# Spreading the inverse softmax sums of two later attentions through DRAM, in a three-part transformer kernel

## What is computed

```python
x = layernorm(x + attn_block(x))          # 16 heads of 16, window 128, then an MLP of 1024
y = x
for l in range(2):                        # the two later layers
    h = shift_token(y)                    # half of the columns come from the token before
    q, k, v = split(h @ wqkv[l], 3)       # 8 heads of 64
    q, k = l2norm(q) * qs[l], l2norm(k) * ks[l]
    q, k = rotary_xpos(q, k)
    o = local_attention(q, k, v)          # softmax over the window before and the window itself
    y = y + o @ wo[l]
    h = layer_norm(shift_token(y)) @ w1[l] + b1[l]
    a, g = split(h, 2)
    y = y + (a * gelu(g)) @ w2[l] + b2[l]
x = layernorm(x + y)
```

## Time and profile before

| | |
|---|---|
| time of the runs | 1791.54 us median of 3 (1789.31 to 1791.67) |
| the profiled execution | span 1791.1 us; its own time is not given apart, the median is 0.4 us above the span |
| TensorE busy | 1731.2 us (97%) |
| VectorE busy | 1494.1 us (83%) |
| ScalarE busy | 1197.5 us (67%) |
| GpSimd busy | 1080.0 us (60%) |
| DMA queue of SyncE | 20.5% of 16 engines' span |
| granted TensorE clock | 9 tenths or more in all slices |

### The profile page before, as it was taken

One profiled execution on the slowest core, in us unless ns is written; L12 is line 12 of the kernel. 1 busy time (PEld: TensorE's weight loads), 2 busy tenths in 40 slices (PEclk: granted clock), 3 DMA queues, 4 the chain that ended last, 5 costly groups with the idle time before them and its releaser, 6 DMA issues.

```text
span 1791.1 us, 43798 instructions
## 1 busy us (share of the span) xinstructions
PE 1731.2 (97%) x15424; PEld 1496.0 (84%) x15424; DVE 1494.1 (83%) x3797; ACT 1197.5 (67%) x3088; POOL 1080.0 (60%) x1060
## 2 busy tenths in 40 slices
PE   6999999999999999999999999989999999999997
PEld 4778777789998888888887888878888888888886
DVE  6888988868878898888987678789898898967776
ACT  6999988854445787877876334358787877743332
POOL 3676556534434778778773455377878777634343
PEclk9999999999999999999999999999999999999999
DMA  3111211032322111111112434331111111131221
GB/s 107 38 37 38 67 44 31 26 107 75 108 63 99 48 41 54 44 52 51 44 43 71 147 105 126 100 103 41 52 44 55 41 54 47 31 102 56 82 82 36
DMA packets 139812, 116.03 MB, mean 65 GB/s; under 512 B 10584, under 2 KB 138848, under 8 KB 138848
## 3 DMA queue, kind: packets, MB, share of 16 engines
q1 hardware_dynamic: 139616, 113.53, 20.5%
HBM read 75.74 MB, written 37.75 MB: 63 GB/s over the span
## 4 chain that ended last, share of the span: by engine, by line
PE 84%; DVE 9%; ACT 3%; issue 3%; POOL 0%; DMA 0%; SPq 0%; DVEq 0%; POOLq 0%; ACTq 0%
PE psum L567 17%; PE psum L569 17%; PE psum L568 17%; PE psum L906 6%; PE psum L874 5%; PE psum L887 5%; PE psum L682 3%; PE psum L664 3%; PE psum L848 3%; ACT a_probs L1718 2%; PE psum L920 2%; PE psum L617 1%; DVE a_neg_max L1211 1%; DVE psum L1209 1%; PE psum L654 1%
## 5 line engine op out<-in xcount | busy, mean ns | idle before, releaser
L1837 ACT ACTIVATE b_probs<-masked,neg_max 128x256 f32<-128x256 f32 (+1 forms) x512 | 250.6, 494 | 124.3 <-DVE neg_max L1343 124.3
L1343 DVE CUSTOM_DVE_ANT_0 masked<-psum,mask 128x256 f32<-128x256 f32 (+1 forms) x512 | 177.3, 412 | 75.9 <-PE psum L874 75.9
L567 PE MATMUL psum<-wa_hi,b_h_hi 128*128 128x512 f32 (+1 forms) x576 | 233.8, 406 | 6.9 <-DVE wa_lo L1138 3.9
L568 PE MATMUL psum<-wa_lo,b_h_hi 128*128 128x512 f32 (+1 forms) x576 | 214.0, 372 | 0.0
L569 PE MATMUL psum<-wa_hi,b_h_lo 128*128 128x512 f32 (+1 forms) x576 | 214.0, 372 | 0.0
L567 PE MATMUL psum<-g_h_hi,wm_hi 128*128 128x512 f32 (+1 forms) x480 | 190.5, 397 | 2.7 <-POOL g_h_lo L2121 1.6
L2070 POOL TENSOR_TENSOR g_in<-g_in,minus_half 128x16 f32<-128x16 f32 x64 | 188.2, 2940 | 4.5 <-DVE g_in L1295 4.5
L568 PE MATMUL psum<-g_h_lo,wm_hi 128*128 128x512 f32 (+1 forms) x480 | 189.3, 394 | 0.0
L569 PE MATMUL psum<-g_h_hi,wm_lo 128*128 128x512 f32 (+1 forms) x480 | 189.2, 394 | 0.0
L1458 POOL TENSOR_TENSOR g_in<-g_z,g_in 128x512 f32<-128x512 f32 x62 | 79.8, 1287 | 143.4 <-DVE g_in L1289 138.2
L567 PE MATMUL psum<-wm_hi,u_hi 128*128 128x256 f32 x576 | 164.3, 285 | 0.1
(11 more groups left out here) (169 smaller groups left out, 5644.0 us busy)
## 6 DMA issues: line engine op xcount, KB each, us to landing
x_mid<-y_out SPq DMA_DIRECT2D x96, 128.0 KB, 1.7
rope_in<-in_rope SPq DMA_DIRECT2D x64, 128.0 KB, 2.2
x_res<-x_state SPq DMA_DIRECT2D x64, 128.0 KB, 2.2
g_in<-x_mid SPq DMA_DIRECT2D x32, 256.0 KB, 3.8
g_old<-x_state SPq DMA_DIRECT2D x16, 512.0 KB, 4.0
out_x<-g_fin SPq DMA_DIRECT2D x15, 512.0 KB, 2.9
w_raw<-in_w_mlp_b SPq DMA_DIRECT2D x2, 2154.0 KB, 8.8
x_in<-in_x SPq DMA_DIRECT2D x32, 128.0 KB, 2.2
```

The lines of the kernel that those rows point to most:

```text
L567: nc.tensor.matmul(out, a_hi, b_hi, start=first, stop=False)
L568: nc.tensor.matmul(out, a_hi, b_lo, start=False, stop=False)
L1343: ins = nc.vector.tensor_tensor_reduce(out[:, at], src[:, at], (mask if now else mask0)[:, at], -1.0, BIG, ALU.add, ALU.min, neg_max[:, r, ...
L1837: ins = nc.scalar.activation(out, src, ACT.Exp, bias=neg_max[:, r, k:k + 1], scale=-1.0, accum_out=row_sum[:, n % 2, 4 * r + k:4 * r + k + 1])
```

## The change

The GpSimd copy, the four transposes and the ScalarE copy are gone, with the tile b_inv_wide and the waits on them. In their place SyncE issues three DMAs a chunk: a store of b_inv to a DRAM tensor inverse_rows with rows of one head's 128 queries (number by number, since the sums lie the other way), and two reads, each of which brings four of the eight rows to 64 partitions. b_inv_t has two buffers now. In chunks 1 to 31 the store stands ahead of the step's output store and the reads behind it; in chunk 0 both stand at the end of the step. VectorE waits for the reads in `scale_o` and for the store in `invert_sums`.

```diff
     x_mid_sh = nc.dram_tensor("x_mid_sh", (TOK + P, P), F32, kind="Internal").ap()
+    inverse_rows = nc.dram_tensor("inverse_rows", (2 * ATT_B.NH, P), F32, kind="Internal").ap()
...
         row_sum = sbuf("row_sum", [P, 2, 8], at=b_ctx)
-        b_inv, b_inv_wide = sbuf("b_inv", [P, 8], at=b_ctx), sbuf("b_inv_wide", [P, 512], at=b_ctx)
-        b_inv_t = sbuf("b_inv_t", [P, 512], at=b_ctx)
+        b_inv = sbuf("b_inv", [P, 8], at=b_ctx)
+        b_inv_t = sbuf("b_inv_t", [P, 2, 4, P], at=b_ctx)
         b_o = sbuf("b_o", [P, 512], at=b_ctx)
...
-            S, g0 = SB, layer * NCH
+            c, S, g0 = ATT_B, SB, layer * NCH
...
+            def inverse_of(n):
+                at = (n % 2) * c.NH
+                return inverse_rows[at:at + c.NH, :]
+            def store_inverse(n):
+                sp.wait_ge(S["inv_ready"], g0 + n + 1)
+                if g0 + n >= 2:
+                    sp.wait_ge(S[f"inv_spread{n % 2}"], 32 * ((g0 + n) // 2))
+                sp.dma_start(inverse_of(n).rearrange("h q -> q h"), b_inv[:], allow_slow_non_contiguous=True).then_inc(S["inv_stored"], 16)
+            def spread_inverse(n):
+                sp.wait_ge(S["inv_stored"], 16 * (g0 + n + 1))
+                if g0 + n >= 2:
+                    sp.wait_ge(S["o_scaled"], g0 + n - 1)
+                for b in range(2):
+                    src = inverse_of(n).rearrange("(t b) q -> b t q", b=2)[b:b + 1, :, :].to_broadcast([c.DH, 4, P])
+                    sp.dma_start(b_inv_t[b * c.DH:(b + 1) * c.DH, n % 2, :, :], src).then_inc(S[f"inv_spread{n % 2}"], 16)
             load_mlp_weights(sp, io["w_mlp_b"][layer * P:layer * P + P, :], layer + 2)
...
                     sp_mlp(sp, MLP_B, MB, layer, opening=True)
+                if b_chunk(s) and s > 0:
+                    store_inverse(s)
                 if b_chunk(s - 2):
                     store(s - 2)
+                if b_chunk(s) and s > 0:
+                    spread_inverse(s)
                 if b_chunk(s):
...
                     sp_mlp(sp, *mlp_behind(layer), None if layer == 0 else layer - 1, opening="last")
+                    store_inverse(0)
+                    spread_inverse(0)
                 if s == 4:
...
                     pe.wait_ge(S["v_copied"], g0 + n - 1)
-                    pe.wait_ge(S["r_copied"], g0 + n - 3)
                 src = x_in[:, n % U, :, :].rearrange("p a d -> p (a d)")
...
                     pe.wait_ge(S["h_lo"], g0 + min(n + 2, NCH))
-                if n >= 3:
-                    pe.wait_ge(S["r_copied"], g0 + n - 2)
                 project(n, 2, (early[0], O, W2)[min(n, 2)])
...
-            def spread_inverse(n):
-                pe.wait_ge(S["inv_wide"], g0 + n + 1)
-                pe.wait_ge(S["v_copied"], g0 + min(n + 3, NCH))
-                if n == NCH - 2:
-                    pe.wait_ge(S["y_ready"], g0 + NCH - 3)
-                if n == NCH - 1:
-                    pe.wait_ge(S["r_copied"], g0 + n)
-                for t in range(4):
-                    mm = nc.tensor.transpose(W2[:, t * P:t * P + P], b_inv_wide[:, t * P:t * P + P], ident[:])
-                mm.then_inc(S["inv_spread"], 1)
             def out_project(n):
                 if n == NCH - 4:
-                    pe.wait_ge(S["r_copied"], g0 + NCH - 2)
+                    pe.wait_ge(S["v_copied"], g0 + NCH)
                 elif n == NCH - 3:
...
                     values(s - 1, 1)
-                    spread_inverse(s - 1)
                 if s == NCH + 1:
...
                 if g0 + n > 0:
-                    v.wait_ge(S["inv_wide"], g0 + n)
+                    v.wait_ge(S["inv_stored"], 16 * (g0 + n))
                 nc.vector.reciprocal(b_inv[:], row_sum[:, n % 2, :]).then_inc(S["inv_ready"], 1)
...
             def scale_o(n):
-                v.wait_ge(S["r_copied"], g0 + n + 1)
+                v.wait_ge(S[f"inv_spread{n % 2}"], 32 * ((g0 + n) // 2) + 32)
                 v.wait_ge(S["pv_done"], 2 * (g0 + n) + 2)
...
                     v.wait_ge(S["o_lo"], g0 + n)
-                nc.vector.tensor_tensor(b_o[:], O[:], b_inv_t[:], ALU.mult).then_inc(S["o_scaled"], 1)
+                nc.vector.tensor_tensor(b_o[:].rearrange("p (t q) -> p t q", q=P), O[:].rearrange("p (t q) -> p t q", q=P),
+                                        b_inv_t[:, n % 2, :, :], ALU.mult).then_inc(S["o_scaled"], 1)
...
-            def copy_spread(n):
-                a.wait_ge(S["inv_spread"], g0 + n + 1)
-                if g0 + n > 0:
-                    a.wait_ge(S["o_scaled"], g0 + n)
-                nc.scalar.activation(b_inv_t[:], W2[:], ACT.Copy).then_inc(S["r_copied"], 1)
             def o_high(n):
...
                     exponentials(s, 0)
-                if b_chunk(s - 1):
-                    copy_spread(s - 1)
                 if b_chunk(s):
...
-            def widen_inverse(n):
-                pool.wait_ge(S["inv_ready"], g0 + n + 1)
-                if n == 0:
-                    pool.wait_ge(zero_rows_stored, layer * 32 + 16)
-                if g0 + n > 0:
-                    pool.wait_ge(S["inv_spread"], g0 + n)
-                nc.gpsimd.tensor_copy(b_inv_wide[:].rearrange("p (h d) -> p h d", d=64),
-                                      b_inv[:].unsqueeze(2).to_broadcast([P, 8, 64])).then_inc(S["inv_wide"], 1)
             if opening:
...
                     rotate_k(s + 2)
-                if b_chunk(s):
-                    widen_inverse(s)
             pool.wait_ge(S["y_ready"], g0 + NCH)
```

More of the change, by code:

```diff
@@ L308, in build @@
             scores_ready max_ready exp_ready pt_ready pt_act pt_dve pv_done
-            inv_ready inv_wide inv_spread r_copied o_scaled o_hi o_lo wo_ready y_ready""")
+            inv_ready inv_stored inv_spread0 inv_spread1 o_scaled o_hi o_lo wo_ready y_ready""")
         mlp_names = """load0 load1 old0 old1 store out_store params stats aggr var rstd z_ready xt_ready h32_ready h_hi h_lo h_lo_pool
```

## The result

| | |
|---|---|
| time of the runs | 2228.36 us median of 4 (2225.11 to 2229.66), before 1791.61 (1789.31 to 1791.92) |
| ratio after to before | 1.2435 [1.2418, 1.2453] |
| the profiled execution | 2228.44 us, span 2226.7 us |
| TensorE, VectorE, ScalarE, GpSimd busy | 83%, 67%, 53%, 47% |
| mean granted TensorE clock | 0.910, before 0.994 |

The forecast was 1783 us and faster; the kernel became 437 us slower, outside the range too.

A forecast was written before the change was run, and what follows sets the result against it. VectorE was taken as nearly as late as TensorE, so TensorE's freed time mostly could not be used. 1791.1 - 10.2 (steady stretch) + 1.7 (layer's end) = 1782.6, given as 1783 us; range 1774 to 1900.

The forecast's parts named there:

- S: Time of each chunk's transposing store to DRAM: 1.32 us fixed plus 64 packets per engine, put at 2.0 us.
- p: Engine time per 4-byte packet of the transposing store, taken as 10.6 ns from the 64-byte rows of vec_a.
- Rival A: Transposing store: 4-byte writes cost more than 1 KB ones, being merged with neighbours; about 1957 us at 100 ns; chance 0.22.
- T: From the reciprocal's end to scale_o in each chunk, through the store and two reads: 5.6 us.
- The estimate beside the sentence of the Trainium skill: Transposing store at a 19-fold loss on 0.68 us: 13 us, 16 from reciprocal to scale_o, run near 2260.
- The cover: Gap of 7.75 us between reciprocal and scale_o hides the DMA chain with 2.1 us to spare.
- The gain if hidden: Ordinary chunk: next scores 0.20 us earlier of TensorE's 0.42, chunks 12.37 apart; steady stretch saves 10.2 us.
- C: Ordinary chunks: DMAs hidden but the 0.16 is VectorE's own, so nothing is gained, 1791.5 us; chance 0.10.
- D: Ordinary chunks: projection needs no fresh start behind b_h_lo, all 0.42 counts, 24 us saved, about 1767; chance 0.03.
- The reads: Two repeated 128 KB reads a chunk: 2.4 us to land, the second issued about 0.47 behind the first.
- The end of a layer: Chunk 30's store behind the next MLP's loads: scale_o 1.7 us later in the first layer, nothing in the second.
- Chunk 31: Last chunk of a layer: gap of 4.48 us, 1.1 short, costed at nothing because VectorE idles 7.64 us behind it.

The follow-up runs named there:

- second experiment: Changed kernel with each stored number in its own 64 bytes and reads taken from a constant (wrong factors): 1795.71 us.
- sixth: Changed kernel with each stored number in 32 bytes of its own, two to 64 bytes, reads from a constant (wrong factors): 1795.52 us.
- seventh: Changed kernel with each stored number in 16 bytes of its own, four to 64 bytes, reads from a constant (wrong factors): 1801.4 us.
- ninth experiment: Changed kernel with stored numbers 8 bytes apart, eight to 64 bytes from eight partitions, reads from a constant (wrong factors): 1867.17 us.
- first experiment: Changed kernel storing b_inv untransposed as 128 rows of 32 bytes (wrong factors), waits and reads kept: 1794.62 us, ratio 1.0017 to the kernel before.
- fifth experiment: Changed kernel with TensorE transposing, ScalarE copying, eight 512-byte rows stored, half the next MLP's first loads behind chunk 30's reads: 1786.39 us, 0.9966 of the original.

## Why the prediction was wrong

**The step that failed is the transposing store's price**, S = 1.32 + 64 p = 2.0 us, with p from the rows nearest in size. S is 10.55. The error is not in p: the engines take 7.4 ns a packet where 10.6 were assumed. The 1.32, the fixed part of a plain store, is what does not carry over: part of it is the time from the last packet to the confirmation, and for sixteen separate writes to each 64 bytes that grows to 8 us (1002.25 to 1010.34). The formula had no term for it. Had the numbers lain 64 bytes apart, S would have been 2.6 and T covered.

**Rival A** (0.22) is what came, with its mechanism as far as the runs can tell: neighbours are what makes it slow, shown by the second, sixth, seventh and ninth experiments; that they are merged is not shown. Its price per packet was in the wrong place. The tail of the range was cut at T = 9.8, and T came out at 14.48. The estimate beside the sentence of the Trainium skill, 13 us for S and a run near 2260, lay close by luck: the same rearranged pattern, as many packets below 512 bytes, takes 2.6 us in the second experiment.

**T and the period.** The cover ends at T = 7.75, and beyond that the period is T + 4.62: T = 14.48 gives 19.10, measured 19.12. From chunk 1 to chunk 30 pass 553.31 and 556.30 us, before 363.27 and 362.97: that makes 383 of the 437 us; the rest is in the first and the last two chunks of the layers, as in chunk 30, where scale_o starts 18.50 and 17.53 us behind the reciprocal. The ninth experiment confirms it between the ends: T = 8.93, so 13.55, measured 13.57.

**The gain if hidden** was right within 0.05 us in an ordinary chunk and within 1.3 us over the steady stretch: 12.42 in the first and fifth experiments against 12.37, and 8.9 us won in the first against 10.2. VectorE bounds the chunk, and TensorE's 0.42 us are mostly lost. Rivals C and D fall with it as to the ordinary chunk. But with the store quick the kernel takes 1794.62 us and not 1783, so the price of the store is not all that failed.

**The reads** were taken as 2.4 us and a second issue 0.47 behind. They land after 3.1, of which 0.3 is the repetition, and the two issues take 1.24 us (first experiment). Where the store is quick, T's cover of 2.1 us swallows that.

**The end of a layer** was mis-sized: 1.7 us in the first and nothing in the second. It is 5.1 and 3.1 us in the first experiment, which is the gain of the steady stretch almost whole. There the store is issued 3.23 us behind the reciprocal, but the reads only 8.42 behind it: the store's confirmation comes late while the next MLP's loads are under way (5.2 and 4.3 us in the two layers, where 1.4 is the median). Chunk 31, taken at nothing because VectorE idles behind it, costs another 1.2 and 1.9. In the fifth experiment, with half of these loads behind the reads, chunk 30 waits for 0.93 and 0 us, but chunk 31 for 3.49 and 1.75.

**What stays open:** what in the memory makes neighbouring writes slow, and whether the size that counts is 64 bytes or another; the runs vary the spacing, and with it the stretch of DRAM that 1024 numbers cover (4 KB in the change, 64 KB in the second experiment). Why the same spacing is slower out of one partition is open too. The fifth experiment changed the store's path and the loads at once, so its 6 us (1786.39 against 1792.47) are not shown for either by itself.

## What to carry to other kernels

A store of single numbers is priced more by where they land than by how many packets it makes: numbers that land side by side from different packets delay the semaphore long after the DMA engines are done, and everything that waits on that semaphore with it. The DMAs issued behind such a store can be held too. Transpose on chip first, or leave gaps, and look in the trace for the time between the last busy DMA window and the release of the waiter. Before a round trip through DRAM is put on a chain, work out how late it may be: here 7.75 us, beyond which each microsecond cost some 64, one a chunk. And look at the ends of a loop as closely as at its middle: here they cost more than the middle won.

## What the runs showed of the hardware

- A DMA's confirmation can outlast its engine time many times over: 1024 packets of 4 bytes took 7.3 to 7.4 ns each in the three stores whose windows are shown (8 and 16 numbers to 64 bytes), and over all spacings the confirmation came after 2.6 to 10.55 us.
- It rises steeply with density: from one to four numbers per 64 bytes 0.6 us more, from eight to sixteen 5.9. Half as many numbers at the full density saved under 2 us.
- Eight numbers to 64 bytes out of one partition took 6.40 us, out of eight partitions 4.62.
- A store that is confirmed late can hold the stores behind it too: the same 192 KB kept the 16 engines for 1.6 us behind the densest store and for 0.6 behind that of the ninth experiment.
- In the slow kernel TensorE's granted clock was 0.50, the 1.2 GHz level, in the stretch behind its wait for b_o, and 0.910 over the whole span where it had been 0.994.
